# Two deformable convolutions: the upper line's scaling moves to ScalarE, and bias and leaky step run for two tiles at a time

## The chip, the cores and the metric

The kernel runs on one core of a Trainium2 chip. The metric is the device time of one execution in microseconds (us), the median of several. TensorE is PE below, VectorE DVE, ScalarE ACT, GpSimd POOL and SyncE SP, as in the profile.

## The reference

The input x is 8 images of 512 channels, 52 x 52 pixels, in float32. Two deformable convolutions follow each other, each with batch norm and leaky ReLU (slope 0.1), and x is added at the end:

```python
def _bilinear(img, y, x):
    ...
    return gather(y0, x0) * (wy0 * wx0)[:, None] + gather(y0, x0 + 1) * (wy0 * wx1)[:, None] + gather(y0 + 1, x0) * (wy1 * wx0)[:, None] + gather(y0 + 1, x0 + 1) * (wy1 * wx1)[:, None]

def _dcnv2(x, w_off, b_off, w, b, k, pad):
    om = lax.conv_general_dilated(x, w_off, (1, 1), [(pad, pad), (pad, pad)])
    ...
    sy = oy + base_y[None]
    sx = ox + base_x[None]
    val = _bilinear(x, sy, sx) * mask[:, None]
    out = jnp.einsum('ncphw,ocp->nohw', val, w.reshape(w.shape[0], C, P))
    return out + b[None, :, None, None]

h = _bn_lrelu(_dcnv2(x, w_off1, b_off1, w1, b1, 1, 0), g1, bb1, m1, v1)
h = _bn_lrelu(_dcnv2(h, w_off2, b_off2, w2, b2, 3, 1), g2, bb2, m2, v2)
return x + h
```

The first has a 1 x 1 kernel (512 to 256 channels), the second a 3 x 3 kernel (256 to 512). Each sampled pixel is a weighted sum of four neighbours.

## The kernel before

The 21632 pixels form 169 tiles of 128 pixels, and 13 tiles form a chunk, of which there are 13. There are three stages, each written for every engine apart; an engine runs its instructions in the order written, and semaphores tie the engines together.

The first stage multiplies x by the first weights (norm folded in) and writes the products y to a table in DRAM, two pixels to a row. The third stage samples h for nine taps and multiplies on PE; it takes from 680 us to the end.

The change lies in the second stage. For each tile t, POOL gathers 1024 values per pixel into one of eight slots of `gather1`: an upper pair of lines (two neighbours of 256 channels) and a second pair. Then:

- `near(t)` on ACT (L768) scales the first 512 values into a PSUM bank;
- `add_far(t)` on DVE (L865) scales the other 512 and adds the bank, which gives two lines of 256, written back to the slot (`lines_ready`);
- `add_upper(t)` on DVE (L881) scales the upper line by `weights1[:, 2, t]` and adds the folded bias, which lies in PSUM (`bias_psum`); the result is the tile of h;
- `add_lower(t)` on DVE (L889) scales the lower line and adds it to h (`sampled1`, which also frees the slot for POOL);
- `activate(pair)` on DVE (L898) takes the leaky step for two tiles (for one at a chunk's end, a chunk having an odd number), and signals `h_ready`.

From h_ready PE transposes the pair (L703), ACT copies it to `h_t` (L776), PE convolves bands of eight image rows for the offsets of the second convolution (L718, three passes), ACT folds each band in three parts (L790), PE turns it back (L736). Once in a chunk ACT keeps a tail (L794), takes the sigmoid (L803) and the hats (L812 to L820), DVE places the samples in a chain of linked steps (L914 to L923, at tile 11) and multiplies by the modulation (L933, at tile 1). ACT also issues the DMAs that write h to the table.

The order on DVE for tile t is add_far(t), add_lower(t - 1), add_upper(t), activate for the pair that ends with t - 1. On ACT it is near(t + 1), copy of h_t for the pair that ends with t - 2, folds, and the steps of the chunk. near(t + 1) waits for add_far(t - 1); add_far(t) waits for near(t).

Of the kernel before, what the change touches and what calls it, by code (L numbers as in the profile page):

```python
# [10 lines left out]
P = 128  # L11
# [28 lines left out]
SLOTS = 8  # L40
# [38 lines left out]
def deformable_kernel(nc, x, w1, norm1, w_off2, w2, norm2_col, b_off1, b_off2, where, tap_at,  # L79
# [16 lines left out]
    with ExitStack() as ctx:  # L96
# [3 lines left out]
        def sem(name):  # L100
            return ctx.enter_context(nc.semaphore(name))
# [476 lines left out]
        def second_stage():  # L578
            gathered = [sem(f"gathered1_{s}") for s in range(SLOTS)]
            near_scaled = sem("near1_scaled")  # L580
            lines_ready = sem("lines1_ready")
            upper_added = sem("upper1_added")
            h_ready = sem("h_ready")
# [171 lines left out]
            def on_scalar(act, begin_unit, begin_upper):  # L755
                def near(t):
# [9 lines left out]
                    if t > NEAR_AHEAD:  # L766
                        act.wait_ge(lines_ready, t - 1)
                    nc.scalar.activation(near_bank(t), gather1[:, t % SLOTS, 0:2 * C_MID], ACT.Identity,  # L768
                                         scale=weights1[:, 0, t:t + 1]).then_inc(near_scaled, 1)

                def copy_h_t(pair):
                    c, j, n = pair_tiles(pair)
                    act.wait_ge(h_transposed, tiles_to(pair))
                    if c:
                        act.wait_ge(convolved, (c - 1) * len(BANDS) + ((j + n) * P - 1) // BAND + 1)
                    nc.scalar.activation(h_t[:, :, j * P:(j + n) * P], pair_bank(pair)[:, :, 0:n * P],  # L776
                                         ACT.Copy).then_inc(h_t_ready, n)
# [46 lines left out]
                def run(late_modulation):  # L824
                    act.wait_ge(const_ready, 1)
                    for t in range(TILES + DRAIN):
                        if NEAR_AHEAD <= t + 1 < TILES:
                            near(t + 1)
                        if t - 2 in PAIR_AT:
                            copy_h_t(PAIR_AT[t - 2])  # L830
# [19 lines left out]
                        if 0 <= t - TILES - 1 < BEGUN:  # L850

                            if t == TILES + 1:
                                act.wait_ge(lines_ready, TILES)
                                act.wait_ge(upper_added, TILES)
                            begin_unit(t - TILES - 1)
# [6 lines left out]
            def on_vector(dve, begin_units):  # L862
# [6 lines left out]

                def add_upper(t):  # L870
                    c, j = divmod(t, CHUNK)
                    for half in range(2):
                        if j == HALVES[half][0] and c == 1:

                            dve.wait_ge(table1_written[half], (CHUNKS + 1) * 32)
                        if j == HALVES[half][0] and c >= 2:

                            dve.wait_ge(table2_written[c % 2][half], written_to(c % 2, c))
                            dve.wait_ge(h_transposed, (c - 2) * CHUNK + HALVES[half][0] + HALVES[half][1])
                    dve.wait_ge(lines_ready, t + 1)  # L880
                    nc.vector.scalar_tensor_tensor(  # L881
                        out=h_buf(c)[:, j, :], in0=gather1[:, t % SLOTS, 0:C_MID],
                        scalar=weights1[:, 2, t:t + 1], in1=bias_psum, op0=ALU.mult, op1=ALU.add)\
                        .then_inc(upper_added, 1)

                def add_lower(t):
                    dve.wait_ge(upper_added, t + 1)
                    v = h_buf(t // CHUNK)[:, t % CHUNK, :]
# [5 lines left out]
                def activate(pair):  # L894
                    c, j, n = pair_tiles(pair)
                    dve.wait_ge(sampled1, tiles_to(pair))
                    v = h_buf(c)[:, j:j + n, :]
                    nc.vector.scalar_tensor_tensor(out=v, in0=v, scalar=SLOPE, in1=v,  # L898
                                                   op0=ALU.mult, op1=ALU.max).then_inc(h_ready, n)
# [36 lines left out]
                def run(late_plan):  # L936
                    dve.wait_ge(bias_ready, 1)
                    for t in range(TILES + 1):
# [4 lines left out]
                        if t:  # L943
                            add_lower(t - 1)
                        if t < TILES:
                            add_upper(t)
                        if t - 1 in PAIR_AT:
# [458 lines left out]
```

## Time and profile before

| | us |
|---|---|
| median of three runs | 3087.31 (3086.87 to 3090.81) |
| the profiled execution | 3092.68 |
| its span, first to last instruction | 3090.7 |
| granted TensorE clock, mean | 0.990 |
| PE busy | 2990.6 (97%) |
| DVE busy | 2740.9 (89%) |
| ACT busy | 2494.6 (81%) |
| POOL busy | 1746.9 (57%) |

The span is what the trace covers; the execution's own time is 2.0 us more. Busy time is the time in which an engine has an instruction running. It tells nothing yet of what sets the time: for this the stretches, the waits and the order in time are read stage by stage. Times in a timeline are microseconds from the span's start.

### The profile page before, as it was taken

Reading aid. Unit: us, or ns where it says so; the run is one execution under the profiler, and the core shown is the slowest. Engines: PE = TensorE matmul, PEld = TensorE weight load, DVE = VectorE, ACT = ScalarE, POOL = GpSimd, SP = SyncE. Lnnn points to the kernel's source line nnn. Section 1 sums busy time; section 2 is a strip of 40 time slices with the busy share of each in tenths; the row PEclk is TensorE's granted clock in tenths of the full one; section 3 lists DMA queues with packets and bytes.
Section 4 is the critical chain, followed back from the end, with each engine's and each line's share of the span. In section 5 each row is a group of like instructions: output and inputs, shape, how many; then the busy total and the mean of one; then the engine's idle time right before and its main releaser. Section 6 shows DMA issues by size and latency. Waiting matters only on the chain.

```text
span 3090.7 us, 49986 instructions
## 1 busy us (share of the span) xinstructions
PE 2990.6 (97%) x15660; PEld 2476.2 (80%) x15660; DVE 2740.9 (89%) x4740; ACT 2494.6 (81%) x4658; POOL 1746.9 (57%) x1701
## 2 busy tenths in 40 slices
PE   6998888889999999999999999999999999999999
PEld 6997455558888888888888888888888888888889
DVE  5545999979999999999999999999999999999988
ACT  4665677778888888888888888888888888888886
POOL 0001444456666666666666666666666666666662
PEclk9999899989999999999999999999999999999999
DMA  9998999999999999999999999999999999999995
GB/s 319 318 341 308 375 353 347 347 348 401 382 369 386 382 370 385 378 373 385 371 378 386 368 380 388 366 383 386 365 386 381 366 378 365 366 379 359 371 368 184
DMA packets 431233, 1123.45 MB, mean 363 GB/s; under 512 B 42844, under 2 KB 171356, under 8 KB 431120
## 3 DMA queue, kind: packets, MB, share of 16 engines
q0 software_dynamic: 244672, 891.09, 76.0%
q1 hardware_dynamic: 118608, 163.05, 14.7%
q10 hardware_dynamic: 67840, 68.16, 6.4%
q8 instruction: 28, 0.46, 0.1%
q14 instruction: 85, 0.70, 0.1%
HBM read 1002.15 MB, written 137.04 MB: 369 GB/s over the span
## 4 chain that ended last, share of the span: by engine, by line
PE 88%; DVE 7%; DMA 1%; ACT 1%; issue 1%; ACTq 1%; SPq 0%; DVEq 0%
PE psum_t L1315 66%; PE psum_t L1302 11%; PE psum_t L394 5%; PE psum_t L718 4%; DVE arena L865 2%; PE psum_t L703 1%; DMA arena<-w 1%; DVE arena L898 1%; DVE arena L889 1%; ACTq L299 1%; PE psum_t L736 1%; DVE val_lo L513 1%; DVE arena L1234 1%; DVE arena L881 0%; ACT val_hi L412 0%
## 5 line engine op out<-in xcount | busy, mean ns | idle before, releaser
L1169 POOL DMA_INDIRECT arena<-table,plan_in x1521 | 1578.2, 1038 | 842.7 <-DVE arena L1242 386.6
L1315 PE MATMUL psum_t<-val_hi,w_hi 128*128 128x512 f32 (+2 forms) x3096 | 1231.4, 398 | 0.0
L1183 ACT ACTIVATE psum_t<-arena,plan_in 128x512 f32<-128x512 f32 x1521 | 1043.5, 686 | 206.8 <-DVE arena L1234 206.7
L1315 PE MATMUL psum_t<-val_hi,w_lo 128*128 128x512 f32 (+2 forms) x3096 | 1198.9, 387 | 0.0
L1315 PE MATMUL psum_t<-val_lo,w_hi 128*128 128x512 f32 (+2 forms) x3096 | 1196.6, 387 | 0.0
L1234 DVE SCALAR_TENSOR_TENSOR arena<-arena,plan_in,psum_t 128x512 f32<-128x512 f32 x1521 | 1135.7, 747 | 32.1 <-ACT psum_t L1183 32.1
L1315 PEld LDWEIGHTS psum_t<-val_hi,w_lo 128*128 128x128 f32 x3096 | 582.0, 188 | 119.2
L1315 PEld LDWEIGHTS psum_t<-val_lo,w_hi 128*128 128x128 f32 x3096 | 584.0, 189 | 103.6
L1315 PEld LDWEIGHTS psum_t<-val_hi,w_hi 128*128 128x128 f32 x3096 | 583.5, 188 | 103.0
L1249 DVE TENSOR_TENSOR val_lo<-psum_t,val_hi 128x1024 fp32r<-128x1024 f32 (+2 forms) x387 | 467.0, 1207 | 147.5 <-ACT val_hi L1197 147.4
L1197 ACT ACTIVATE val_hi<-psum_t 128x1024 fp32r<-128x1024 f32 (+2 forms) x387 | 388.0, 1002 | 154.1 <-PE psum_t L1302 153.8
L1191 ACT ACTIVATE arena<-arena,plan_in 128x256 f32<-128x256 f32 x1014 | 503.5, 497 | 0.1
L1242 DVE SCALAR_TENSOR_TENSOR arena<-arena,plan_in 128x256 f32<-128x256 f32 x1014 | 492.6, 486 | 0.0
L690 POOL DMA_INDIRECT arena<-table,arena x169 | 163.8, 969 | 405.5 <-DMA table<-arena 214.0
L1302 PE MATMUL psum_t<-ident,arena 128*128 128x128 f32 x2028 | 264.3, 273 | 9.1 <-DVE arena L1242 8.9
L1302 PEld LDWEIGHTS psum_t<-ident,arena 128*128 128x128 f32 x2028 | 237.5, 141 | 41.6 <-issue 8.7
L1191 ACT ACTIVATE val_first<-arena,plan_in 128x256 f32<-128x256 f32 x507 | 254.1, 501 | 0.1
L1242 DVE SCALAR_TENSOR_TENSOR val_first<-arena,plan_in,val_first 128x256 f32<-128x256 f32 x507 | 245.3, 484 | 0.0
L718 PE MATMUL psum_t<-arena 128*96 128x408 f32 (+1 forms) x624 | 239.6, 522 | 0.0
L394 PE MATMUL psum_t<-w_hi,val_hi 128*128 128x260 f32 x676 | 200.3, 296 | 37.6 <-DVE val_lo L513 37.3
L513 DVE TENSOR_TENSOR val_lo<-arena,val_hi 128x512 fp32r<-128x512 f32 x169 | 115.7, 691 | 126.8 <-ACT val_hi L412 126.7
L394 PE MATMUL psum_t<-w_lo,val_hi 128*128 128x260 f32 x676 | 195.3, 289 | 0.0
(90 smaller groups left out, 2406.9 us busy)
## 6 DMA issues: line engine op xcount, KB each, us to landing
arena<-x SPq DMA_DIRECT2D x90, 512.0 KB, 8.5
table<-arena ACTq DMA_DIRECT2D x40, 896.0 KB, 8.3
out<-arena SPq DMA_DIRECT2D x136, 256.0 KB, 5.7
table<-arena ACTq DMA_DIRECT2D x40, 768.0 KB, 6.9
arena<-x SPq DMA_DIRECT2D x70, 384.0 KB, 6.3
arena<-table,plan_in POOLq DMA_INDIRECT x1521, 7.0
table<-table SPq DMA_DIRECT2D x32, 512.0 KB, 11.6
arena<-w POOLq DMA_DIRECT2D x2, 2304.0 KB, 13.7
```

The costliest lines, as they stand in the source:

```text
L394: last = nc.tensor.matmul(y_bank(j), a[:, X_SLOT[j], k, :], b[:, k, :], start=(k == 0 and a is x_hi and b is w1_hi), stop=(k == KT1 - 1 an ...
L690: nc.gpsimd.indirect_dma_start(gather1[:, t % SLOTS, :], None, table1[0:image_end(t) + WIDTH, :], bass.IndirectOffsetOnAxis(ap=index1[:, t ...
L718: last = nc.tensor.matmul(out_rows[:, :, to:to + w], woff_sb[:, kt, dx, :], h_rows[:, :, at:at + w], start=(nth == 0 and kt == 0), stop=(n ...
L1169: nc.gpsimd.indirect_dma_start(landing(r, i)[:, :], None, rows, bass.IndirectOffsetOnAxis(ap=row.bitcast(u32), axis=0))\
L1183: nc.scalar.activation(psum_near[:, unit(r, i) % NEARS, :], landing(r, i)[:, 0:2 * C_MID], ACT.Identity, scale=weight(r, i, 0)).then_inc(n ...
L1191: nc.scalar.activation(val(r, i), landing(r, i)[:, 0:C_MID], ACT.Identity, scale=weight(r, i, 2)).then_inc(line_scaled, 1)
L1197: nc.scalar.activation(val_hi[:, r % 2, :, 0:n], psum_val[:, :, 0:n], ACT.Identity).then_inc(hi_ready, 1)
L1234: nc.vector.scalar_tensor_tensor(out=landing(r, i)[:, 0:2 * C_MID], in0=landing(r, i)[:, 2 * C_MID:4 * C_MID], scalar=weight(r, i, 1), in1 ...
L1242: nc.vector.scalar_tensor_tensor(out=v, in0=landing(r, i)[:, C_MID:2 * C_MID], scalar=weight(r, i, 3), in1=v, op0=ALU.mult, op1=ALU.add).t ...
L1249: nc.vector.tensor_tensor(val_lo[:, r % 2, :, 0:n], psum_val[:, :, 0:n], val_hi[:, r % 2, :, 0:n].bitcast(f32), ALU.subtract)\
L1302: last = nc.tensor.transpose(psum_val[:, kt, i * P:(i + 1) * P], val(r, i)[:, kt * P:(kt + 1) * P], ident[:, :])
L1315: last = nc.tensor.matmul(psum_acc[:, oc, 0:n], a[:, w, oc * P:(oc + 1) * P], b[:, r % 2, kt, 0:n], start=(w == 0 and a is w2_hi and b is ...
```

## The change

The upper line is scaled by ACT, in a new function `scale_upper(t)` that stands right behind near(t + 1) in ACT's order and takes over all the waits of add_upper; it writes the scaled line to h without the bias. DVE's add_upper is gone; add_lower waits for `upper_scaled` instead. In activate, DVE first adds the bias to the two tiles (one instruction, the bias broadcast over the tiles), waits for that, and then takes the leaky step. In the third stage's beginning ACT waits for upper_scaled in place of upper_added.

```diff
+                def scale_upper(t):
+                    c, j = divmod(t, CHUNK)
+                    for half in range(2):
+                        if j == HALVES[half][0] and c == 1:
+
+                            act.wait_ge(table1_written[half], (CHUNKS + 1) * 32)
+                        if j == HALVES[half][0] and c >= 2:
+
+                            act.wait_ge(table2_written[c % 2][half], written_to(c % 2, c))
+                            act.wait_ge(h_transposed, (c - 2) * CHUNK + HALVES[half][0] + HALVES[half][1])
+                    act.wait_ge(lines_ready, t + 1)
+                    nc.scalar.activation(h_buf(c)[:, j, :], gather1[:, t % SLOTS, 0:C_MID], ACT.Identity,
+                                         scale=weights1[:, 2, t:t + 1]).then_inc(upper_scaled, 1)
...
                         if NEAR_AHEAD <= t + 1 < TILES:
                             near(t + 1)
+                        if t < TILES:
+                            scale_upper(t)
                         if t - 2 in PAIR_AT:
                             copy_h_t(PAIR_AT[t - 2])
...
-                                act.wait_ge(upper_added, TILES)
+                                act.wait_ge(upper_scaled, TILES)
...
-                def add_upper(t):
...
-                    dve.wait_ge(lines_ready, t + 1)
-                    nc.vector.scalar_tensor_tensor(
-                        out=h_buf(c)[:, j, :], in0=gather1[:, t % SLOTS, 0:C_MID],
-                        scalar=weights1[:, 2, t:t + 1], in1=bias_psum, op0=ALU.mult, op1=ALU.add)\
-                        .then_inc(upper_added, 1)
-
                 def add_lower(t):
-                    dve.wait_ge(upper_added, t + 1)
+                    dve.wait_ge(upper_scaled, t + 1)
...
                     dve.wait_ge(sampled1, tiles_to(pair))
                     v = h_buf(c)[:, j:j + n, :]
+                    nc.vector.tensor_tensor(v, v, bias_psum.unsqueeze(1).to_broadcast([P, n, C_MID]), ALU.add)\
+                        .then_inc(bias_added, 1)
+                    dve.wait_ge(bias_added, pair + 1)
                     nc.vector.scalar_tensor_tensor(out=v, in0=v, scalar=SLOPE, in1=v,
                                                    op0=ALU.mult, op1=ALU.max).then_inc(h_ready, n)
...
                             add_lower(t - 1)
-                        if t < TILES:
-                            add_upper(t)
```

## Rows read from the trace of the kernel before

**Rows 1.** The page: busy time of each engine, its share of the span, instructions.
```profile
PE 2990.6 (97%) x15660; PEld 2476.2 (80%) x15660; DVE 2740.9 (89%) x4740; ACT 2494.6 (81%) x4658; POOL 1746.9 (57%) x1701
```

**Rows 2.** Table of stretches: start and end, length, busy time of each engine, clock, DMA.
```profile
core 0: us, PE busy (x) PEld busy (x) DVE busy (x) ACT busy (x) POOL busy (x), PEclk, DMA share, GB/s
295.00:640.00 345.00, 298.46 (x1289) 173.45 (x1289) 329.08 (x711) 256.37 (x534) 162.31 (x168) 0.96 0.96 347
...
398.00:424.00 26.00, 23.18 (x97) 13.20 (x96) 24.62 (x54) 19.16 (x41) 12.19 (x13) 0.93 0.99 355
577.50:603.00 25.50, 22.86 (x101) 13.11 (x100) 25.11 (x55) 20.20 (x42) 12.56 (x13) 1.00 0.97 346
...
680.00:3040.00 2360.00, 2359.83 (x11928) 1988.00 (x11927) 2202.84 (x3671) 2016.46 (x3507) 1543.38 (x1486) 1.00 0.99 376
```

**Rows 3.** Waits, 300 to 636 us: who waited for whom; total us, times, longest.
```profile
ACT arena L790 <- PE psum_t L718: 43.5, 48, 1.5
...
ACT arena L776 <- issue: 20.1, 36, 1.7
...
DVE arena L865 <- ACT psum_t L768: 10.3, 17, 4.6
```

**Rows 4.** Timeline of DVE in one chunk: start, duration, engine, line, operation [idle before].
```profile
577.49 0.75 DVE L865 SCALAR_TENSOR_TENSOR arena<-arena,psum_t 128x512 f32<-128x512 f32 x1 [0.22 <-ACT psum_t L768]
578.16 0.48 DVE L889 SCALAR_TENSOR_TENSOR arena<-arena 128x256 f32<-128x256 f32 x1
578.55 0.48 DVE L881 SCALAR_TENSOR_TENSOR arena<-arena,psum_t 128x256 f32<-128x256 f32 x1
578.94 0.68 DVE L898 SCALAR_TENSOR_TENSOR arena<-arena 128x512 f32<-128x512 f32 x1
579.54 0.74 DVE L865 SCALAR_TENSOR_TENSOR arena<-arena,psum_t 128x512 f32<-128x512 f32 x1
...
602.93 0.75 DVE L865 SCALAR_TENSOR_TENSOR arena<-arena,psum_t 128x512 f32<-128x512 f32 x1 [0.22 <-ACT psum_t L768]
```

**Rows 5.** The same timeline: two steps of the plan's chain.
```profile
584.48 0.40 DVE L914 TENSOR_TENSOR arena<-psum_t,arena 128x234 f32<-128x234 f32 x1
584.91 0.28 DVE L917 TENSOR_SCALAR arena<-arena 128x234 f32<-128x234 f32 x1
```

**Rows 6.** Groups by line and form: busy us, mean ns of one, idle before.
```profile
L1249 DVE TENSOR_TENSOR val_lo<-psum_t,val_hi 128x1024 fp32r<-128x1024 f32 x369 | 452.2, 1225 | 136.4 <-ACT val_hi L1197 136.3
...
L1266 DVE TENSOR_TENSOR arena<-z_sb,arena 128x512 f32<-128x512 f32 x164 | 113.8, 694 | 0.0
...
L898 DVE SCALAR_TENSOR_TENSOR arena<-arena 128x256 f32<-128x256 f32 x13 | 5.5, 419 | 0.0
```

**Rows 7.** Timeline of ACT in the third stage: the scaling of 256 elements.
```profile
1002.72 0.50 ACT L1191 ACTIVATE arena<-arena,plan_in 128x256 f32<-128x256 f32 x1
1003.12 0.68 ACT L1183 ACTIVATE psum_t<-arena,plan_in 128x512 f32<-128x512 f32 x1
```

**Rows 8.** Timeline of ACT at a chunk's turn.
```profile
586.20 0.51 ACT L790 ACTIVATE arena<-psum_t 32x416 f32<-32x416 f32 x1
...
588.67 0.67 ACT L768 ACTIVATE psum_t<-arena 128x512 f32<-128x512 f32 x1
589.42 0.60 ACT L776 ACTIVATE arena<-psum_t 128x512 f32<-128x512 f32 x1
590.74 0.51 ACT L790 ACTIVATE arena<-psum_t 32x416 f32<-32x416 f32 x1 [0.72 <-PE psum_t L718]
...
591.15 0.67 ACT L768 ACTIVATE psum_t<-arena 128x512 f32<-128x512 f32 x1
```

**Rows 9.** Timeline of DVE: first and last row of a chunk at a lower clock.
```profile
397.43 0.75 DVE L865 SCALAR_TENSOR_TENSOR arena<-arena,psum_t 128x512 f32<-128x512 f32 x1 [0.39 <-ACT psum_t L768]
...
424.53 0.75 DVE L865 SCALAR_TENSOR_TENSOR arena<-arena,psum_t 128x512 f32<-128x512 f32 x1 [0.39 <-ACT psum_t L768]
```

More of the change, by code:

```diff
@@ L581, in second_stage @@
             lines_ready = sem("lines1_ready")
-            upper_added = sem("upper1_added")
+            upper_scaled = sem("upper1_scaled")
+            bias_added = sem("bias1_added")
             h_ready = sem("h_ready")
@@ L868, in add_far @@
                         .then_inc(lines_ready, 1)
-                def add_upper(t):
[L871 to L879, printed above, removed]
-                    dve.wait_ge(lines_ready, t + 1)
-                    nc.vector.scalar_tensor_tensor(
-                        out=h_buf(c)[:, j, :], in0=gather1[:, t % SLOTS, 0:C_MID],
-                        scalar=weights1[:, 2, t:t + 1], in1=bias_psum, op0=ALU.mult, op1=ALU.add)\
-                        .then_inc(upper_added, 1)
                 def add_lower(t):
-                    dve.wait_ge(upper_added, t + 1)
+                    dve.wait_ge(upper_scaled, t + 1)
                     v = h_buf(t // CHUNK)[:, t % CHUNK, :]
```

## The prediction

> **What bounds the kernel now.** I read the shares of the span first: TensorE is busy for 97%, VectorE 89%, ACT 81% [rows 1]. Such averages hide the stages, so the next view is the table of stretches [rows 2]. From 680 us on (the third stage) PE is busy for 2359.83 of 2360 us: it sets the time there, and nothing in the change touches it. The second stage, 295 to 640 us, is another matter: VectorE is busy for 329.08 of 345 us, PE for 298.46, ACT for 256.37. In an even chunk of it (577.5 to 603 us) VectorE is busy for 25.11 us, ACT for 20.20. The third view is that of the waits [rows 3]: in the whole second stage the large addition on VectorE waits 10.3 us for ACT, of which one wait is 4.6; ACT waits 43.5 us for the convolution on PE and 20.1 us before the copies of the transposed h. So VectorE is the bound, ACT has free time, and a good part of that is time in which ACT stands at the convolution. The last view is the order in time on VectorE [rows 4]: a chunk of 13 tiles runs from 577.49 to 602.93, 25.44 us, of which 0.22 is a wait. A microsecond that a chunk gains or loses moves the end by 13 us, since the third stage starts when the second has given out its plan and its gather buffers.
>
> **What leaves VectorE.** Unlinked VectorE instructions start before the one ahead has ended, so I count from start to start [rows 4]: the far line takes 0.67 (577.49 to 578.16), the lower line 0.39 (to 578.55), the upper line 0.39 (to 578.94), the leaky step of two tiles 0.60 (to 579.54). The upper line leaves: 13 x 0.39 = 5.1 us a chunk.
>
> **What comes to VectorE.** No row shows the addition of the broadcast bias to two tiles. Its bounds are a tensor-tensor of 512 elements in SBUF, 0.694 us, and one of 1024 with an operand in PSUM, 1.225 us [rows 6]; it has 512 elements, and before the change the upper line read this same bias at the same pace as the lower line reads SBUF (0.39 each) [rows 4]. I take 0.69. It is also linked on both sides: it waits for the lower line just ahead of it, between which and the leaky step the upper line stood before, and the leaky step waits for it. What a link costs is seen in the chain of the plan [rows 5]: a step of 0.40 us is followed after 0.43 (584.48 to 584.91), 0.03 to 0.04 behind its end, where an unlinked one starts about 0.08 ahead of the end (0.75 long, next after 0.67) [rows 4]. So the lower line ahead of it counts 0.48 + 0.04 = 0.52 instead of 0.39, and the bias 0.69 + 0.04 = 0.73: 0.86 more for a pair, against 2 x 0.39 = 0.78 removed, +0.08. Six pairs give +0.4 to +0.5. The single last tile of a chunk loses 0.39 and gains 0.13 + 0.46 (256 elements, from its leaky step of 0.419 [rows 6]): +0.2. VectorE's own work grows by **0.6 us a chunk**, 8 us in all, though it has given a third of its additions away. Behind the new wait stand the next far and lower lines; the transposes on PE wait for the leaky step, which ends some 0.5 us later after its far line.
>
> The Trainium skill (VectorE: DVE Perf Modes, The DRAIN you can't avoid) says of chained VectorE instructions that a semaphore between them costs nothing extra. By that a pair would be 0.78 out and 0.61 in, a gain of about 1 us a chunk; [rows 5] against [rows 4] show 0.11 to 0.12 for each link, so I go by the rows.
>
> **What comes to ACT.** The same form exists in the third stage: 128x256, scaled by a column, SBUF to SBUF, 0.50 us, the next one starting 0.40 later [rows 7]. 13 x 0.40 = 5.2 us a chunk, at most 13 x 0.50 = 6.5 where nothing overlaps. ACT is busy for 20.20 of 25.5 us [rows 2], so its work becomes 25.4 and more: as much as the whole chunk takes today, before a single wait. Moreover scale_upper(t) waits for the far line t, whereas near(t + 1), so far ACT's tightest tie, waits for far line t - 1 only. Behind this wait stand the copy of h_t, the folds and the next near line, for which PE and VectorE wait. ACT thus can no longer do folds and copies ahead of time.
>
> **The two together.** I laid one chunk out, in two columns with the steps above, ACT's from [rows 8]. The place that decides is the chunk's turn. Count from the start of far line 12 (586.50 us before). Its end is 0.75, so scale_upper(12) runs from 0.78 to 1.28. The fold starts at 1.31; from this fold to near line 1 of the next chunk are 588.67 - 586.20 = 2.47 us (the hats) [rows 8], so near 1 starts at 3.78 and ends at 4.45. VectorE, after 2.51 (step 12: 0.67 + 0.52 + 0.73 + 0.60) and 1.97 (step 0), wants it at 4.48: in time. Then ACT does scale_upper(0) 4.39 to 4.89, the copy to 5.49, the fold 5.52 to 6.03, and near 2 from 5.94 to 6.61. VectorE has far line 1, lower line 0 and the modulation behind it, 1.44, and wants near 2 at 5.92: it waits 0.7. Before, near 2 stood at 591.15, 4.65 after far line 12 [rows 8], and was there in time. The same reckoning gives 0.25, 0.37 and 0.37 at three later steps (those with a fold that waits for PE or two folds in a row), 1.7 in all. So the chunk is 25.2 + 0.6 + 1.7 = 27.5; the copies and scalings in it were put end to end, and by up to 0.09 each less where they overlap it is 27.1. I take **27.1, +1.7 us a chunk**, 13 chunks: +22 us.
>
> Costed at nothing: the removed wait of the third stage's beginning, now on ACT's own count; the gather slots, which are still freed by the lower line right behind the far line of the next tile; the table's DMAs on ACT's queue, which stand behind one more scaling (the last of them well ahead of its need). The profiled execution has a span of 3090.7, with 2.0 around it, and is 5.4 above the median. 3090.7 + 22 + 2.0 - 5.4 = 3109.3 us, **3109**.
>
> **Rivals.** (a) *VectorE's sum alone.* ACT fits its work into its free time and the waits for PE shrink as ACT comes later to them: +0.6 x 13 = +8, 3095; with a bias add that links more cheaply it falls within 0.2%, which is about what a measurement of this kernel can tell from no change (6 us). For it: ACT's sum of 25.4 is under 25.8. Against it: no free time is left for the waits. 0.14, and 0.10 for a loss of under 6 us. (b) *Faster.* If links cost nothing, VectorE sheds 1.0 us a chunk, and if ACT keeps up, the time is 3087 - 13 = 3074. It takes over where ACT's scaling costs under 0.32 us ((24.4 - 20.2) / 13); the row says 0.40. 0.04. (c) *PE's clock joins in.* In 398 to 424 us the granted clock was 0.93, and the chunk from 397.43 to 424.53 took 27.10 instead of 25.44 [rows 2, 9], as ACT and with it VectorE waited longer for PE. PE stands idle more often after the change, and ACT has nothing left to absorb it. With 1.66 more in every chunk: +22 + 22 = +44, 3131. 0.14. (d) *The change is not what binds*, since PE hides it: [rows 2] leave PE 2.6 us free a chunk, but the waits are VectorE's, so this has no weight beyond (a).
>
> **Chances and range.** The forecast (+12 to +36, mostly 3100 to 3123) gets 0.58; (a) 0.24, (b) 0.04, (c) 0.14. Faster 0.04 (b), same 0.10 (the smaller loss in (a)), slower 0.86. The low end is VectorE's sum with somewhat cheaper links, 3093; the high end reaches to (c), 3133.
>
> **What the profile after would show.** The first part right: the bias add at 0.69 us, starting 0.03 to 0.05 behind the lower line's end; a pair of about 3.58 us on VectorE where nothing waits. The second: ACT busy for over 94% of a chunk, its wait for PE in the folds well under 43.5 us, and VectorE's wait for near lines up from 10.3 to 20 to 30 us. The chunks at 27 us; the third stage unchanged and later by 22. Wrong it would be if the scaling overlaps with its neighbours more than 0.1 us, if ACT shows waits that VectorE does not feel, or if chunks stay at 25.8.

## The result, and the profile after

The changed kernel takes **3122.96 us** (median of four, 3120.84 to 3124.50); the kernel before, on the same chip, 3089.06 (3086.87 to 3092.66). The ratio is 1.0107, 95% interval 1.0095 to 1.0120. The forecast was 3109 in a range of 3093 to 3133. The profiled execution took 3122.72, with a span of 3120.8. The first lines of its page, to be held against [rows 1]:

```profile
span 3120.8 us, 50078 instructions
...
PE 2996.3 (96%) x15660; PEld 2471.4 (79%) x15660; DVE 2744.5 (88%) x4662; ACT 2567.1 (82%) x4827; POOL 1763.0 (56%) x1701
```

VectorE has 78 instructions fewer and is busy 3.6 us longer; ACT has 72.5 us more. Neither share says where the time went. The table of stretches does: a chunk of the second stage (compare 577.5 to 603 in [rows 2]) and the third stage. Its columns are start and end, length, busy time and count of PE, PEld, DVE, ACT and POOL, granted clock, DMA share and GB/s.

```profile
547.45:574.91 27.46, 23.19 (x101) 12.99 (x100) 25.48 (x50) 26.04 (x56) 13.56 (x13) 1.00 0.96 336
...
680.00:3040.00 2360.00, 2345.30 (x11798) 1966.74 (x11799) 2190.64 (x3653) 2002.67 (x3493) 1548.34 (x1483) 1.00 0.99 376
```

There are **two losses**. A chunk now takes 27.46 us instead of 25.44, with ACT busy for 26.04 of it. And in the third stage, which the change hardly touches, PE is idle for 14.7 of 2360 us where it was idle for 0.17 (a part of this is the stage's beginning, which now reaches into the window).

To size them I take marks on VectorE that both traces have. From the first chunk's first place instruction (`place`, L914 before, L918 after) to the twelfth's it was 351.41 to 635.37, 283.96 us; now it is 352.49 to 655.11, 302.62: +18.7 over 11 chunks. The first far line of the third stage moves from 643.54 to 663.82, +20.3. From there to the end of the span it was 2447.2 us and is 2457.0: **+9.8**. Together 30.1, the growth of the span; the medians differ by 33.9, because the profiled execution of before lay 3.6 above its median and that of after on it.

The waits of the second stage, 300 to 660 us, to be held against [rows 3] (who waited for whom; total, times, longest):

```profile
ACT arena L783 <- DVE arena L882: 14.8, 18, 2.9
...
DVE arena L882 <- ACT psum_t L769: 9.6, 24, 1.2
```

ACT's wait for the convolution, 43.5 us before, has gone down to 4.0. The waits of the third stage, 700 to 3120 us:

```profile
DVE arena L1236 <- ACT psum_t L1185: 69.1, 62, 2.8
ACT psum_t L1185 <- issue: 62.2, 18, 3.7
...
PE psum_t L1304 <- DVE arena L1244: 7.0, 18, 0.6
```

The line in the middle is what I had not foreseen: 18 times ACT stands for up to 3.7 us at its first scaling, while the profile names nothing it waits for. VectorE's wait for this line is 69.1 us where the trace of before shows 23.6, and PE waits for VectorE behind it. One of the 18, in the timelines of ACT and of VectorE:

```profile
1011.77 0.50 ACT L1193 ACTIVATE arena<-arena,plan_in 128x256 f32<-128x256 f32 x1
1015.92 0.69 ACT L1185 ACTIVATE psum_t<-arena,plan_in 128x512 f32<-128x512 f32 x1 [3.65 <-issue]
```
```profile
1016.64 0.75 DVE L1236 SCALAR_TENSOR_TENSOR arena<-arena,plan_in,psum_t 128x512 f32<-128x512 f32 x1 [2.72 <-ACT psum_t L1185]
```

They come 114.8 us apart (900.91, 1015.92, 1130.78 to 2852.45). ACT's third stage is a loop over 299 instructions that jumps back 18 times, and that is its period. Below, a turn is one such jump back. The list of DMA queues has a second sign. After:

```profile
q14 instruction: 175, 1.43, 0.1%
```

The page of before has 85 there: 90 more packets on a queue that carries instructions, five for each of 18 turns.

### The profile page after: what moved, and what is told of

It is laid out like the page before. It is cut to its first block, busy times and chain, and to the rows that moved or that the text cites. A ratio compares the mean times of both kernels' runs of the same rounds, so it can differ in the third digit from the quotient of the medians.

```text
span 3120.8 us, 50078 instructions
## 1 busy us (share of the span) xinstructions
PE 2996.3 (96%) x15660; PEld 2471.4 (79%) x15660; DVE 2744.5 (88%) x4662; ACT 2567.1 (82%) x4827; POOL 1763.0 (56%) x1701
## 4 chain that ended last, share of the span: by engine, by line
PE 59%; DVE 24%; ACT 9%; issue 6%; DMA 1%; ACTq 1%; DVEq 0%; SPq 0%
PE psum_t L1317 44%; PE psum_t L1304 7%; DVE arena L1236 7%; PE psum_t L394 5%; DVE val_lo L1251 4%; DVE arena L1244 2%; ACT arena L1193 2%; DVE arena L882 2%; DVE val_first L1244 2%; DVE z_sb L1258 1%; DVE arena L1268 1%; PE psum_t L719 1%; ACT psum_t L769 1%; ACT val_hi L1199 1%; ACT psum_t L1185 1%
## 5 line engine op out<-in xcount | busy, mean ns | idle before, releaser
L691 POOL DMA_INDIRECT arena<-table,arena x169 | 172.7, 1022 | 415.6 <-DMA table<-arena 213.5
L394 PE MATMUL psum_t<-w_hi,val_lo 128*128 128x260 f32 x676 | 195.6, 289 | 0.0
```

Source lines behind the costliest of these rows:

```text
L394: last = nc.tensor.matmul(y_bank(j), a[:, X_SLOT[j], k, :], b[:, k, :], start=(k == 0 and a is x_hi and b is w1_hi), stop=(k == KT1 - 1 an ...
L691: nc.gpsimd.indirect_dma_start(gather1[:, t % SLOTS, :], None, table1[0:image_end(t) + WIDTH, :], bass.IndirectOffsetOnAxis(ap=index1[:, t ...
```

## The experiments

The questions are: does the loop's stall come from the change or from where the change puts ACT's code, and what makes the chunk longer, VectorE's own work, ACT's load, or how the two are tied together. The ratio given with a run is to the kernel before on the same chip. Times of different experiments are held against each other only where the kernel before takes 3089.1 to 3090.4 us; one chip, on which it takes 3289.64, is named where it comes up. A chunk is measured from one `place` to the next.

### The changed kernel with ACT's code shifted

Counted from ACT's first instruction (the loop that ACT has in the first stage counted once), the loop begins at instruction 1388 before and at 1582 after. In blocks of 256 instructions these are 108 and 46 past a block's start. 62 semaphore increments on ACT ahead of all work put it at 1644, which is 108 past a start again.

```diff
+            spare = sem("spare")
...
+                for _ in range(62):
+                    act.sem_inc(spare, 1)
```

> The changed kernel with 62 more semaphore increments on ACT ahead of its first instruction that waits, so that the body of ACT's loop in the third stage lies at the same place within a block of 256 instructions as in the kernel before (1644 and 1388 counted instructions ahead of it; they differ by 256). Theory A (the third stage's extra 10 us come from where ACT's loop lies in its code: 18 stalls of ACT of 2.9 to 3.7 us, 115 us apart, each at the loop's turn): the stalls vanish, the third stage takes as long as before, the total falls by 8 to 11 us, to about 3113. Theory B (the third stage suffers from what the second leaves behind, as buffers or transfers that stand otherwise): the stalls stay, about 3123. In both the second stage stays as in the changed kernel, chunks of 27.4 us.

Measured: 3111.70 us (3110.69 to 3112.24), ratio to before 1.0074 (1.0056 to 1.0092), span 3109.1. No stall is left, the instruction queue has 86 packets, and VectorE's wait is what it was before, to the digit:

```profile
DVE arena L1239 <- ACT psum_t L1188: 23.6, 44, 1.0
```

The chunks stay at 27.15 to 27.76 us, apart from one of 28.94 at a granted clock of 0.94. So of the 33.9 us some 11 (3122.96 less 3111.70) belong to the loop's stalls and 22 to the second stage.

### The kernel before with ACT's code shifted

The reverse: before, with 194 increments among ACT's instructions of the first stage, so that its loop begins at 1582.

```diff
+                        if (first or plans or last) and j < 11:
+                            for _ in range(4):
+                                act.sem_inc(spare, 1)
...
+                for _ in range(62):
+                    act.sem_inc(spare, 1)
```

> The kernel before with 194 more semaphore increments on ACT in the first stage (62 at its start, 132 spread over three of its chunks), which put the loop of the third stage at the same place as in the changed kernel (1582 counted instructions ahead of it in both). Theory A: 18 stalls of ACT of about 3.5 us appear in the third stage, PE loses 0.4 to 0.5 us at each, total 3089 + 8 to 11 = 3097 to 3100, and whatever the increments cost in the first stage, up to 5 us. Theory B: nothing but that cost, at most 3094.

Measured: 3100.14 us (3096.89 to 3104.02), ratio 1.0035 (1.0023 to 1.0047), +10.3 us. The chunks at full clock are at 25.44, with single ones of 25.6, and the first far line of the third stage stands at 644.41, as before; from there to the end of the span it is 2457.6 us, against 2447.2 before, 2457.0 in the changed kernel and 2446.7 in the shifted one. The table of stretches gives what PE loses, 7.4 us or 0.4 a turn, and the waits show the stalls:

```profile
680.00:3040.00 2360.00, 2352.61 (x11864) 1976.67 (x11863) 2192.24 (x3652) 2003.03 (x3491) 1538.89 (x1480) 1.00 0.99 375
```
```profile
ACT psum_t L1189 <- issue: 63.2, 18, 4.0
```

The same 18 stalls and the same loss, without any of the change's work. It is the position of ACT's code.

### Two more positions

The kernel before with 64 increments (the loop at 1452, 172 past a block's start) and with 162 (at 1550, 14 past; 54 of them at the start, 108 in three chunks of the first stage).

```diff
+                for _ in range(64):
+                    act.sem_inc(spare, 1)
```

> The kernel before with 64 semaphore increments at ACT's start, which put the loop of its third stage at 172 within a block of 256 counted instructions (before 108, changed 46). If only some placements stall (a body of 299 instructions that touches three blocks instead of two), this one shows no stall and the time of the kernel before, 3087 to 3094. If every placement but the old one stalls, 3099.

> Computes everything. The kernel before with 162 semaphore increments on ScalarE ahead of the loop, which then begins at its 1550th instruction. The loop turns of the third stage stalled with the loop at 1582 and at 1452 and not at 1388 and 1644. If only where the loop lies in blocks of 256 instructions counts, and what stalls is a start in either half other than near 108, this placement (14 over a whole block) is a new point: theory 1 (placement in blocks of instructions) gives either 18 stalls of 2.8 to 3.7 us and 3097 to 3102 us or none and 3088 to 3092, and does not say which; theory 2 (any instructions added to the front of the kernel before make the loop stall) gives stalls and 3097 to 3102.

Measured, one execution each: 3095.65 for the first beside 3090.38 for before on that chip, with 18 stalls and 175 packets. Its second stage, which has the instructions of before, was 7.2 us quicker (first far line of the third at 636.36): none of its chunks ran below full clock, where before had three. So a single profile's total can't be held against another's to a few us. But from there to the end it is 2457.1 us, the same +9.9 as in the other stalling kernels:

```profile
ACT psum_t L1186 <- issue: 63.0, 18, 3.8
```

The second has no wait over 0.8 us at that line, and 86 packets. Its time, 3300.98, is no argument: it ran on another chip, where the kernel before takes 3289.64 (3278.36 to 3307.45). So 46 and 172 stall, 14 and 108 don't. My first idea was that the loop stalls where its 299 instructions reach into a third block; none of these four does. The rule that separates them is **open**.

### ACT's third stage written out

If the turn back is what costs, a third stage without a turn should lose nothing wherever its code lies.

```diff
-                return begin_unit, lambda: upper(0, 0), lambda: position(act, step, after=5, first=2)
+                return begin_unit, lambda: upper(0, 0), lambda: in_full(step, after=5, first=2)
```

> Computes everything. The changed kernel with ScalarE's third stage written out instead of looping over 18 taps, so ScalarE takes no branch back there. Theory 1 (the turn of ScalarE's loop, by where its code lies, costs the third stage some 9.8 us): no stall of 2.9 to 3.7 us in that stage, first far line of it still near 663, time 3110 to 3114, that is 9 to 12 us below the changed kernel. Theory 2 (the third stage is longer because of what the second leaves behind, its data or its clock): 3120 to 3125, with VectorE waiting as often for ScalarE's first eviction of a tap. If long straight code stalls by itself, waits of ScalarE for nothing named show spread over the stage, and the time lies above 3114.

Measured: 3287.72 us (3278.63 to 3303.60), on the other chip named above: ratio 0.9996 (0.9974 to 1.0018). At the line that stalled no wait over 1.1 us is left between 700 and 3220 us. But as a time this is inconclusive. On that chip the third stage is not bound by PE, so neither a stall nor a late start need show there. The stretch 1000 to 2000 us of a kernel with before's stage (the one with the links between the tiles, below), in the columns of the table of stretches:

```profile
1000.00:2000.00 1000.00, 947.48 (x4635) 775.52 (x4633) 857.77 (x1431) 783.46 (x1363) 603.73 (x580) 0.99 0.95 348
```

PE is busy for 947 of 1000 us, where in before, on the chip of its profile, it is busy for all 1000. The clean look at the edit is in the last experiment.

### Without the bias addition

The changed kernel, shifted as in the first experiment, less one VectorE instruction and its link for each pair. It leaves the bias of the first convolution out of h.

```diff
-                    nc.vector.tensor_tensor(v, v, bias_psum.unsqueeze(1).to_broadcast([P, n, C_MID]), ALU.add)\
-                        .then_inc(bias_added, 1)
-                    dve.wait_ge(bias_added, pair + 1)
```

> e1 without the bias addition and its wait (the bias of the first convolution is left out of the result): the leaky step follows the lower line, one link remains. VectorE loses 0.80 us a pair (0.51 for the last single tile), 5.2 us a chunk, so its own work is 26.3 - 5.2 = 21 us. Theory 1 (ACT is as full as VectorE: 26.0 busy of 27.46 us a chunk): the chunk falls by no more than 1.5 us, to 26 to 26.5, and the total by 12 to 20 us, to 3094 to 3101, still above the kernel before. Theory 2 (VectorE's longer work alone makes the loss): the chunk falls below 25.4 us, and the total below 3087.

Measured: 3097.68 us (3094.64 to 3101.28), ratio 1.0027 (1.0018 to 1.0037). One chunk of 26.49 us, the mean of those at full clock, in the table of stretches, and VectorE's wait for near lines, 300 to 660 us:

```profile
538.26:564.75 26.49, 22.75 (x102) 13.12 (x101) 21.41 (x42) 25.74 (x56) 12.25 (x13) 1.00 0.99 348
```
```profile
DVE arena L885 <- ACT psum_t L772: 55.1, 99, 5.0
```

VectorE is busy for 21.4 of 26.5 us and waits 55.1 us for near lines. With VectorE relieved of 4 us a chunk, the chunk is still 1.05 longer than before the change. I take that as **ACT's own length**: 25.74 busy, plus what it must still wait for. It is an upper bound, since ACT waits for far lines here too.

### ACT relieved

The reverse: the same kernel, with the scaling reduced to 16 of 256 columns (0.29 to 0.31 us each instead of 0.50). The other 240 columns of the upper line are left out of h.

```diff
-                    nc.scalar.activation(h_buf(c)[:, j, :], gather1[:, t % SLOTS, 0:C_MID], ACT.Identity,
+                    nc.scalar.activation(h_buf(c)[:, j, 0:16], gather1[:, t % SLOTS, 0:16], ACT.Identity,
```

> e1 with ACT's new scaling cut to 16 of 256 columns (the other columns of h take whatever lay there), so that it costs ACT some 0.2 us less each, 2.6 us a chunk, while VectorE does all that it does in the changed kernel. Theory 1: what is left is VectorE's own work with its links, 25.2 + 0.6 + 0.4 (the link behind the bias addition is 0.11 us, not 0.04) = 26.2 us a chunk, total 3089 + 13 x 0.8 = 3099 to 3102. If ACT's load alone made the loss, the chunk would be back at 25.4 to 25.6 and the total at 3090. If VectorE alone made it, nothing changes against e1: 27.4.

Measured: 3107.66 us (3107.24 to 3111.59), ratio 1.0065 (1.0046 to 1.0084). This missed my expectation. The table of stretches shows the two kinds of chunk behind it:

```profile
486.70:514.80 28.10, 24.57 (x101) 13.89 (x100) 25.28 (x50) 23.70 (x56) 13.88 (x13) 0.94 0.92 312
514.80:541.50 26.70, 22.98 (x101) 13.01 (x100) 25.21 (x50) 23.22 (x56) 13.00 (x13) 1.00 0.94 323
```

At full clock the chunk is 26.7 us, with VectorE busy for 25.21, and the rest its links' gaps and what waits are left (10.8 us for near lines in the whole stage; 0.4 in this chunk, by starts that are late). Without them it is 26.3: **VectorE's own length**, where before it was 25.1. Three of the chunks ran at a granted clock of 0.94 and took 28.07 to 28.18, 1.4 more; ACT waited for PE in the folds again (25.8 us). So this run says what VectorE's part is, in the chunks at full clock, but its total overstates it.

### The kernel before, with the load on ACT alone

Before, where ACT scales each upper line too, into a scratch tile that nobody reads, and the lower line on VectorE waits for it. VectorE's instructions are those of before. With 174 increments ahead, the loop is at 1900, 108 past a start.

```diff
+                def scale_upper(t):
+                    act.wait_ge(lines_ready, t + 1)
+                    act.wait_ge(upper_scaled, t)
+                    nc.scalar.activation(scratch[:, :], gather1[:, t % SLOTS, 0:C_MID],
+                                         ACT.Identity, scale=weights1[:, 2, t:t + 1]).then_inc(upper_scaled, 1)
...
+                        if t < TILES:
+                            scale_upper(t)
...
+                    dve.wait_ge(upper_scaled, t + 1)
```

> The kernel before, VectorE's arithmetic untouched (the upper line with its bias stays there), and in addition ACT scales every upper line into a scratch buffer at the place where the changed kernel does it; the lower line waits for that too. ACT's third-stage loop lies at the same place within a block of 256 instructions as in the kernel before. Theory 1 (ACT's load makes most of the loss): chunks of 26.2 to 26.8 us, as without the bias addition, and a total of 3098 to 3103. Theory 2 (VectorE's links and bias make it): chunks of at most 25.7 us, total at most 3093.

Measured: 3108.75 us (3107.47 to 3110.96), ratio 1.0055 (1.0038 to 1.0071). The chunks are 26.68 to 27.56, five of them below full clock. One at full clock:

```profile
407.56:434.61 27.05, 23.03 (x101) 13.04 (x100) 25.65 (x56) 25.82 (x56) 12.56 (x13) 1.00 0.97 349
```

The six at full clock take 26.93 on average: 1.45 us a chunk more than before with not one VectorE instruction changed. The expectation had 26.2 to 26.8 and a total of 3098 to 3103, both too low. The load and the tie are enough for most of the loss; here VectorE's own length is 25.1 and ACT's at most the 26.5 of the run without bias addition, and the chunk is longer than either. At 1900 the loop doesn't stall: from the third stage's first far line to the end it is 2447.8 us.

### Two other orders

First, the scaling behind the copy and the folds in ACT's order, so that near line, copy and fold come early again. Second, on VectorE, the next far line between the bias addition and the leaky step, so that other work covers the link. Both are the changed kernel, shifted.

```diff
-                        if t < TILES:
-                            scale_upper(t)
                         if t - 2 in PAIR_AT:
                             copy_h_t(PAIR_AT[t - 2])
...
+                        if t < TILES:
+                            scale_upper(t)
```

> e1 with the scaling of the upper line moved behind the copy of h_t and the folds of its step on ACT. If the tie counts (ACT waits for far line t before it may copy and fold), the chunk falls from 27.4 to 26.6 to 27.0 and the total to 3101 to 3107. If only the amount of ACT's work counts, it stays at 27.3 to 27.6 and 3111, or becomes slower where the lower line now waits behind a fold that waits for PE (up to 28 us, 3119).

Measured: 3156.39 us (3151.13 to 3157.85), ratio 1.0204 (1.0187 to 1.0222); chunks of 30.6 to 30.8 at full clock and up to 32.5 below it. The wait that replaces the others is the lower line's for the scaling:

```profile
DVE arena L893 <- ACT arena L786: 50.8, 58, 2.1
```

The lower line stands right behind a far line, so the scaling is the more urgent work by far, and a fold ahead of it stops VectorE.

```diff
-                            activate(PAIR_AT[t - 1])
+                            activate(PAIR_AT[t - 1], lambda: far_early(t + 1))
```

> e1 with the far line of the next tile put between the bias addition and the leaky step on VectorE, so that the leaky step is no longer linked to the instruction ahead of it. It takes off 0.11 + 0.08 us at six pairs and some 0.1 at the single tile, 1.2 us of VectorE's 26.2 a chunk. If VectorE's own work sets the chunk, it falls by 1.2 to 26.2 and the total to 3096; if ACT's load does, it falls to no less than the 26.5 of the kernel without the bias addition, total 3099 to 3103; between both lies the reading that each holds up the other.

Measured: 3135.36 us (3132.26 to 3140.15), ratio 1.0139 (1.0122 to 1.0156); three chunks of 28.6 to 28.8 at full clock, eight of 29.7 to 30.6 below it.

```profile
DVE arena L885 <- ACT psum_t L772: 42.2, 70, 1.7
ACT arena L808 <- PE psum_t L722: 29.4, 40, 1.4
```

The link is covered (the far line starts 0.61 to 0.63 behind the bias addition's start), but the leaky step now stands behind a far line that waits for near, near stands behind a fold that waits for PE, and PE waits for the leaky step of a pair. This ring of waits, as I read it, costs more than the 0.1 us it was to save: 1.3 us a chunk at full clock (28.7 against 27.4), and in most chunks the lower clock comes on top. Both expectations missed, for one reason: I priced the edit on its own engine and not what queues behind it.

### The kernel before, with its links covered

What the link rows say can be used where the kernel has links already. The plan's chain (six instructions once in a chunk) is spread, each step behind the next VectorE instruction of a tile.

```diff
                         if FAR_AHEAD <= t < TILES:
                             add_far(t)
+                            one_step()
                         if t:
                             add_lower(t - 1)
+                            one_step()
...
                         if j == 11 and c:
-                            place(c - 1)
+                            steps += place_steps(c - 1)
+                            one_step()
```

> Computes everything. The kernel before, with the second stage's plan chain (six short VectorE instructions, each waiting for the one ahead) no longer in one run but one after each of the next VectorE instructions of the tiles, so that the 0.11 to 0.19 us which each link waits for the one ahead is covered by other work. Theory: a chunk of the second stage falls from 25.45 by 0.5 to 0.6 us, 11 chunks, so 3082 to 3085 us, since VectorE is the busiest engine there and ScalarE and TensorE have slack; ScalarE's code is unchanged, so its loop does not stall. Rival: a chain step stands ahead of a far or lower line and delays TensorE's next transposes by its own 0.1 to 0.5 us, or the plan lands later; then the chunk stays at 25.4 and the time within 3087 to 3091.

Measured, on the chip where before takes 3289.64: 3282.54 us (3277.79 to 3286.40), ratio 0.9976 (0.9959 to 0.9992). To see it where PE binds the third stage, I ran it together with the written-out third stage of ACT:

> Computes everything. The kernel before with both edits: the plan chain of the second stage spread one instruction at a time between the tiles' VectorE instructions, and ScalarE's third stage written out instead of looping. Each is read from its own stage. Second stage: theory 1 (covered links) gives chunks of 24.8 to 24.9 us at full clock against 25.45, so about 6 to 7 us less by the first far line of the third stage. Third stage, on a chip where the kernel before takes about 3089: theory 1 (written out, ScalarE neither gains nor loses where its loop did not stall) gives 2446 to 2449 us from that line to the end of the span, as before, and 3081 to 3084 in all; theory 2 (the straight code stalls by itself, or the longer program is fetched at a cost) gives waits of ScalarE for nothing named and more than 2452 from that line on.

Measured: **3080.92 us** (3078.11 to 3084.80) beside 3090.18 for before (3086.32 to 3095.81), ratio 0.997 (0.9959 to 0.998). A chunk in the table of stretches, and two steps of the chain in VectorE's timeline:

```profile
528.90:553.74 24.84, 23.03 (x102) 13.07 (x101) 24.62 (x56) 20.00 (x44) 13.20 (x13) 1.00 1.03 371
```
```profile
504.08 0.40 DVE L920 TENSOR_TENSOR arena<-psum_t,arena 128x234 f32<-128x234 f32 x1
504.39 0.74 DVE L865 SCALAR_TENSOR_TENSOR arena<-arena,psum_t 128x512 f32<-128x512 f32 x1
505.05 0.28 DVE L932 TENSOR_SCALAR arena<-arena 128x234 f32<-128x234 f32 x1
505.24 0.48 DVE L889 SCALAR_TENSOR_TENSOR arena<-arena 128x256 f32<-128x256 f32 x1
```

A step of 0.40 takes 0.31 of VectorE's time instead of 0.43 [rows 5], one of 0.28 takes 0.19. Seven of the nine chunks at full clock are 24.82 to 24.84, 0.61 less. The first far line of the third stage stands at 635.37, 8.2 earlier; the profile of the kernel with 64 increments has it 7.2 earlier without this edit, so the 0.61 a chunk is the firm number, some 7 us in 11 or 12 chunks. From there to the end it is 2445.4 us, against 2447.2 before and 2445.5 to 2447.8 in the other kernels whose loop doesn't stall: written out, ACT's stage shows no stall of its own, and no gain that stands out. This version is 9.3 us faster than the kernel before on its chip, and the chunks account for most of it.

## Why the prediction was right or wrong

**What binds where: right.** VectorE and ACT set the chunk, PE the third stage.

**VectorE's own work: right in sign, mis-sized.** The timeline of VectorE after, at the start of a chunk:

```profile
574.91 0.74 DVE L882 SCALAR_TENSOR_TENSOR arena<-arena,psum_t 128x512 f32<-128x512 f32 x1
575.57 0.48 DVE L890 SCALAR_TENSOR_TENSOR arena<-arena 128x256 f32<-128x256 f32 x1
576.08 0.69 DVE L899 TENSOR_TENSOR arena<-arena,psum_t 128x512 f32<-128x512 f32 x1
576.88 0.70 DVE L902 SCALAR_TENSOR_TENSOR arena<-arena 128x512 f32<-128x512 f32 x1
577.50 0.73 DVE L882 SCALAR_TENSOR_TENSOR arena<-arena,psum_t 128x512 f32<-128x512 f32 x1
578.16 0.47 DVE L890 SCALAR_TENSOR_TENSOR arena<-arena 128x256 f32<-128x256 f32 x1
578.67 0.42 DVE L899 TENSOR_TENSOR arena<-arena,psum_t 128x256 f32<-128x256 f32 x1
579.12 0.43 DVE L902 SCALAR_TENSOR_TENSOR arena<-arena 128x256 f32<-128x256 f32 x1
```

The addition lasts 0.69, as taken from its nearer bound, and starts 0.03 behind the lower line's end. But the leaky step starts 0.80 behind the addition's start, 0.11 behind its end, where I put 0.04. A pair is 3.63 us, not 3.58, against 3.50 before. The single tile is 1.30 from its lower line to the next far line, against 1.11, the +0.2 of the prediction. From start to start a chunk has 1.07 us more of VectorE's own work; I had 0.6. The 0.04 came from the plan's chain, whose steps are 234 elements wide. The gap of 0.11 stands before the leaky step of two tiles; before that of a single tile it is 0.03 (578.67 to 579.12). What makes it is seen in the run without the bias addition, where the same lower line (256 wide) comes ahead of both:

```profile
567.42 0.48 DVE L893 SCALAR_TENSOR_TENSOR arena<-arena 128x256 f32<-128x256 f32 x1
568.01 0.69 DVE L902 SCALAR_TENSOR_TENSOR arena<-arena 128x512 f32<-128x512 f32 x1
...
569.28 0.48 DVE L893 SCALAR_TENSOR_TENSOR arena<-arena 128x256 f32<-128x256 f32 x1
569.80 0.43 DVE L902 SCALAR_TENSOR_TENSOR arena<-arena 128x256 f32<-128x256 f32 x1
```

The two-tile step starts 0.11 behind the lower line's end, the one-tile step 0.04. So the gap goes with the instruction that waits and not with the one it waits for; and not with the width of 512 alone, for the bias addition has that width too and starts 0.03 behind.

The Trainium skill (VectorE: DVE Perf Modes, The DRAIN you can't avoid) reports of eight chained copies that a semaphore behind each costs nothing extra. For the instructions of this case the rows decide otherwise: an unlinked follower starts 0.08 ahead of the end, a linked one 0.03 to 0.11 behind it, and covering five links gave 0.61 us a chunk.

**ACT's load: right.** The scaling lasts 0.50 us and ACT is busy for 26.04 of 27.46 us, 95%. Its wait in the folds is 4.0 us where 43.5 stood.

**The two together: right in place, nearly right in size.** The wait at the chunk's turn is there, 0.43 where I had 0.7:

```profile
581.41 0.75 DVE L882 SCALAR_TENSOR_TENSOR arena<-arena,psum_t 128x512 f32<-128x512 f32 x1 [0.43 <-ACT psum_t L769]
```

Three more of 0.18, 0.17 and 0.30 follow at 588.96, 592.86 and 596.89, where I had 0.25, 0.37 and 0.37. Counted as starts that are late against an unhindered one (which are 0.08 more than the idle time listed), VectorE loses 1.4 us to near lines in the chunk from 572.89 to 600.52, against 0.3 before. So +1.1 of waits and +1.1 of own work: 27.63 us. My hand-made layout said 27.5, with 0.5 too little own work and 0.3 too much waiting, which nearly cancel; I then took 0.4 off it for overlaps of ACT, which was a correction the chip did not make. The view of waits did not rise to 20 to 30 us, as I had said it would: it fell from 10.3 to 9.6. But of the 10.3, 4.9 fall before the first chunk measured (a single wait of 4.6) and 3.5 into the three chunks below full clock; in the eight at full clock it is 1.9. After, it is 7.0 from 381 us to the stage's end, all at full clock. **A total of waits over a stage hides a tie that costs a few tenths at a time**; the same stretches at the same clock, and starts against starts, are the test.

Chunks at full clock are 27.17 to 27.75, +1.7 to +2.3. The average over 11 is +1.7 because before had three chunks at a granted clock of 0.92 to 0.94 (26.10, 26.92 and 27.09 us), 3.8 us more than at full clock, and after one (28.85), 1.5 more. The forecast's +1.7 a chunk and +22 in all is what the shifted kernel shows (3111.70, +21.8), partly by this: a full-clock chunk costs 1.9 more, not 1.7. That part of the agreement is luck.

What the experiments add is how the two meet. The 11 chunks of each profile, from `place` to `place`:

| kernel | mean chunk at full clock, us | chunks below full clock |
|---|---|---|
| before | 25.48 | 3 |
| changed | 27.38 | 1 |
| changed, without bias addition | 26.49 | 1 |
| changed, ACT relieved | 26.77 | 4 |
| before, load on ACT alone | 26.93 | 5 |
| changed, scaling behind the folds | 30.68 | 5 |
| changed, far line between | 28.69 | 8 |
| before, links covered (and ACT's third stage written out) | 24.87 | 2 |

With ACT relieved the chunk is 26.8, with VectorE relieved 26.5, with both loaded 27.4. The last 0.6 us is, by this difference, the price of the tie between two engines with no slack.

**"The third stage unchanged and later by 22": wrong.** Later by 20.3 is right; unchanged is not. +9.8 us in the span, 11.3 in the median, come from ACT's loop. The step that failed is "nothing in the change touches it": the 194 more instructions that ACT has ahead of its loop move the loop, and that had no term in the sum. Without it the time would have been 3111.7, 2.7 from the forecast, of which 1.8 is the median of before (3087.31 when the forecast was made, 3089.06 beside the result); with it, it was 14 off, inside the range by the room left for rival (c), another case. That is luck, not foresight.

**The rivals.** VectorE's sum alone (3095) is refuted by the load on ACT alone, which costs 18 us with VectorE's work untouched. Faster is refuted by the link rows. PE's clock joining in every chunk did not happen, one chunk of after was at a lower clock; but the price of 1.66 was about right: 1.4 us a chunk in the run with ACT relieved. In the kernel with the far line between, eight of 11 chunks were below full clock.

## What to carry to other kernels

Work moved to an engine that "has room" is worth nothing if it makes that engine as full as the bound one: two engines that would need at most 26.8 and 26.5 us, and wait for each other in every tile, took 27.4. Count a link between two VectorE instructions of the kinds seen here as 0.11 to 0.19 us of its time, and put an independent instruction of the same engine between them, provided that this one never waits. Compare chunks at the same granted clock before comparing totals. After an edit that changes how many instructions an engine has ahead of a loop, look for stalls with no cause named at the loop's turn before believing the reasons for the rest.

## What was not expected of the hardware

ACT's loop of 299 instructions stalls 2.9 to 3.7 us at each of its 18 turns (up to 4.0 in another run) when it begins at ACT instruction 1582 or 1452, and not at 1388, 1550, 1644 or 1900. With each stalling turn go five more packets on the instruction queue. It costs 10 to 11 us of 3090, though the stalls add up to 62: PE loses 0.4 us at a turn, so the work that VectorE and PE have ahead covers most of a stall. The Trainium skill (Runtime: NRT & Kernel Launch, Instruction fetch mechanics) has a branch stall where its target is outside the two blocks of 256 instructions that an engine holds. The packets agree with a fetch at the turn. By the count above each of the six loops lies in two blocks, so this condition alone doesn't tell those that stall. Which blocks are held at which placement, and so why two of six starts stall, no run here settles.

The granted clock of PE was 0.91 to 0.97 of full speed on average in single chunks of most runs. It is not a small step down: in before, PE ran at half speed, the lower of its two levels (1.2 instead of 2.4 GHz), for 3.4 us of one such chunk and at full speed for the rest. A stretch of the table:

```profile
382.77:386.18 3.41, 3.41 (x8) 1.50 (x7) 2.96 (x8) 1.84 (x5) 1.82 (x2) 0.50 1.06 406
```

Such a chunk was up to 1.7 us longer in before, though PE is not the bound there (busy for 24.27 of 27.09 us in one). Folds, transposes and the bound engine wait for each other in turn, which is how I read it; the run with ACT relieved, where ACT waits for PE in the folds again, fits. How many chunks it hits differs from none (before with 64 increments) to eight of 11, and with it the total of a profile by several us.
